# Layer 0's dense stage: the smaller of norm and limit multiplied into the dots in PSUM, not into the cells in SBUF

## What is computed

```python
Wh = h @ W + b
row, col = (edge_index[0], edge_index[1])
sc = jax.nn.softplus(deg_coeff[0] * deg_v + deg_coeff[1])
dot = jnp.sum(Wr * Wc, axis=-1)          # Wr = Wh[row], Wc = Wh[col]
sim = dot / jnp.maximum(nr * nc, EPS)
sim_pos = jax.nn.relu(sim)
sim_neg = -jax.nn.relu(-sim)
base = adj_v * sc * no_diag
prop_pos = jax.ops.segment_sum((base * sim_pos)[:, None] * Wc, row, num_segments=n_nodes)
prop_neg = jax.ops.segment_sum((base * sim_neg)[:, None] * Wc, row, num_segments=n_nodes)
return scale * (coeff[0] * prop_pos + coeff[1] * prop_neg + coeff[2] * Wh)
```

## Time and profile before

| | before |
|---|---|
| median of 3 runs | 5141.49 us (5140.48 to 5144.65) |
| the profiled execution, own time | 5139.28 us |
| its span | 5137.5 us |
| busy PE / DVE / ACT / POOL | 2720.2 / 3940.7 / 789.2 / 3541.7 us |
| chain that ended last, by engine | POOL 39%, issue 19%, PE 17%, DVE 13%, DMA 8% |
| chain, by line, L735 (`add0`) | 16% |

### The profile page before, as it was taken

The page is one execution under the profiler, slowest core; times in us unless marked ns, Lnnn a source line. Parts: engine busy times, 40 slices in busy tenths (PEclk is TensorE's granted clock), DMA queues, the critical chain, the costliest instruction groups (busy, mean ns, idle before and its releaser), DMA issues.

```text
span 5137.5 us, 62046 instructions
## 1 busy us (share of the span) xinstructions
PE 2720.2 (53%) x10695; PEld 1352.5 (26%) x10695; DVE 3940.7 (77%) x10565; ACT 789.2 (15%) x2017; POOL 3541.7 (69%) x3645
## 2 busy tenths in 40 slices
PE   5844266436775000013544444456787777729992
PEld 4532122104665000002211111132333333313331
DVE  8866999646999986646777777755788878789993
ACT  0000022210000025521222222220000000003331
POOL 4777777754777877777777777756777777715562
PEclk9999987668999555557677766678889998869996
DMA  9420167413222146635888888837999999928980
GB/s 350 147 90 9 46 225 256 143 64 118 54 52 54 41 136 203 202 88 197 277 286 290 284 281 287 289 124 252 311 310 305 311 310 311 308 96 311 331 317 21
DMA packets 458298, 1038.77 MB, mean 202 GB/s; under 512 B 129582, under 2 KB 247830, under 8 KB 428141
## 3 DMA queue, kind: packets, MB, share of 16 engines
q1 hardware_dynamic: 167594, 579.38, 31.4%
q0 software_dynamic: 131968, 217.09, 15.0%
q10 hardware_dynamic: 158658, 241.42, 13.5%
HBM read 559.03 MB, written 476.15 MB: 201 GB/s over the span
## 4 chain that ended last, share of the span: by engine, by line
POOL 39%; issue 19%; PE 17%; DVE 13%; DMA 8%; DVEq 1%; ACT 1%; POOLq 0%; SPq 0%; ACTq 0%
POOL arena L696 22%; POOL weights L735 16%; DMA arena<-tab,ring 7%; PE psum L1308 6%; PE psum L1309 5%; PE psum L1389 3%; DVE arena L2242 1%; DVE arena L1698 1%; DVE arena L2069 1%; DVE arena L1963 1%; DVE arena L2073 1%; DVE arena L2055 1%; DVE arena L1848 1%; DMA ring<-meta 1%; DVE arena L2171 1%
## 5 line engine op out<-in xcount | busy, mean ns | idle before, releaser
L696 POOL DMA_INDIRECT arena<-tab,ring x2352 | 2311.3, 983 | 717.3 <-issue 701.5
L1308 PE MATMUL psum<-arena,ident 128*128 128x512 f32 x1176 | 745.2, 721 | 799.6 <-DMA arena<-tab,ring 523.6
L1698 DVE SCALAR_TENSOR_TENSOR arena<-arena,ns 128x64 f32<-128x64 f32 (+2 forms) x2351 | 870.0, 370 | 192.9 <-ACT arena L934 53.0
L735 POOL DMA_INDIRECT weights<-arena x784 | 805.4, 1027 | 291.4 <-issue 238.7
L1309 PE MATMUL psum<-arena,ident 128*128 128x512 f32 x1176 | 687.8, 671 | 0.0
L1308 PEld LDWEIGHTS psum<-arena,ident 128*128 128x128 f32 x1176 | 251.7, 227 | 1184.0 <-issue 993.2
L805 POOL TENSOR_TENSOR arena<-arena,score 128x256 f32<-128x256 f32 x294 | 230.6, 809 | 256.8 <-issue 125.0
L1389 PE MATMUL psum<-arena,ident 128*128 128x512 f32 x784 | 361.4, 607 | 63.9 <-DVE arena L2242 63.5
L2171 DVE SCALAR_TENSOR_TENSOR arena<-psum,rowb 128x1024 f32<-128x1024 f32 x196 | 239.1, 1220 | 200.7 <-PE psum L1309 200.1
L1309 PEld LDWEIGHTS psum<-arena,ident 128*128 128x128 f32 x1176 | 262.7, 223 | 357.4 <-issue 357.4
L1272 PE MATMUL psum<-agg,arena 128*128 128x200 bf16 x2352 | 236.6, 251 | 118.5 <-DVE arena L1821 118.5
(11 more groups left out here) (416 smaller groups left out, 4131.9 us busy)
## 6 DMA issues: line engine op xcount, KB each, us to landing
put<-zero SPq DMA_DIRECT2D x98, 1040.0 KB
arena<-put SPq DMA_DIRECT2D x98, 1040.0 KB
spill<-arena ACTq DMA_DIRECT2D x98, 1024.0 KB, 5.7
arena<-spill SPq DMA_DIRECT2D x98, 1024.0 KB
state<-arena ACTq DMA_DIRECT2D x147, 512.0 KB, 4.7
weights<-zero SPq DMA_DIRECT2D x32, 1600.0 KB, 18.4
arena<-weights SPq DMA_DIRECT2D x32, 1600.0 KB, 7.6
put<-zero SPq DMA_DIRECT2D x14, 3584.0 KB
```

The costliest lines, as they stand in the source:

```text
L696: pool.indirect_dma_start(out=rows[:, h, k, :], out_offset=None, in_=table[:, :], in_offset=bass.IndirectOffsetOnAxis(ap=ring[:, h, word + ...
L735: pool.indirect_dma_start(out=weights0[:, :], out_offset=bass.IndirectOffsetOnAxis(ap=words0[:, g, k:k + 1], axis=0), in_=words0f[:, g, K ...
L1308: pe.matmul(place, lhsT=ident[:, :], rhs=rows_of[0][:, s, columns, 0:width], start=True, stop=False)
L1698: beats.add(dve.scalar_tensor_tensor(out=rows[:, s, k, :], in0=before, scalar=mark(ns, g, k), in1=rows[:, s, k, :], op0=ALU.mult, op1=ALU. ...
```

## The change

The multiplication by the smaller of `per_src` and `limit` is moved from the cells to the dots. The instruction keeps its form and its size; its second tensor and its output are now the PSUM banks with the bent dots. It stands behind `bend0` of the same quarter and waits for it, and `similarity0` waits for it. The wait for the loaded cells moves from the first `weigh0` of a tile to the first `similarity0`.

```diff
-            def weigh0(at, c):
-
-                place, columns = at % 3, slice(c * NP // 4, (c + 1) * NP // 4)
-                if c == 0:
-                    dve.wait_ge(cells_in[place], at // 3 * 16 + 16)
-                dve.scalar_tensor_tensor(out=cells[:, place, columns], in0=per_src[:, columns], scalar=limit[:, ORDER[at]:ORDER[at] + 1],
-                                         in1=cells[:, place, columns], op0=ALU.min, op1=ALU.mult).then_inc(weighted, 1)
-
...
+            def weigh0(at, c):
+
+                dve.wait_ge(bent, at * 4 + c + 1)
+                dve.scalar_tensor_tensor(out=dots_of(c), in0=halves_of(per_src[:, c * NP // 4:(c + 1) * NP // 4]), scalar=limit[:, ORDER[at]:ORDER[at] + 1],
+                                         in1=dots_of(c), op0=ALU.min, op1=ALU.mult).then_inc(weighted, 1)
 
             def similarity0(at, c):
 
-                weights = cells[:, at % 3, c * NP // 4:(c + 1) * NP // 4].rearrange("p (b n) -> p b n", b=2)
+                weights = halves_of(cells[:, at % 3, c * NP // 4:(c + 1) * NP // 4])
+                if c == 0:
+                    dve.wait_ge(cells_in[at % 3], at // 3 * 16 + 16)
                 dve.wait_ge(weighted, at * 4 + c + 1)
-                dve.wait_ge(bent, at * 4 + c + 1)
                 dve.tensor_tensor(weights, weights, dots_of(c), ALU.mult).then_inc(work0, 1)
 
             for at in range(TILES):
-                weigh0(at, 0)
                 for c in range(4):
                     bend0(at, c)
-                    if c < 3:
-                        weigh0(at, c + 1)
+                    weigh0(at, c)
                     similarity0(at, c)
```

More of the change, by code:

```diff
@@ L1738, in _, with halves_of @@
                 tally.done(dve.tensor_copy(weights, bias), wa_set)
-            def weigh0(at, c):
-                place, columns = at % 3, slice(c * NP // 4, (c + 1) * NP // 4)
-                if c == 0:
-                    dve.wait_ge(cells_in[place], at // 3 * 16 + 16)
-                dve.scalar_tensor_tensor(out=cells[:, place, columns], in0=per_src[:, columns], scalar=limit[:, ORDER[at]:ORDER[at] + 1],
-                                         in1=cells[:, place, columns], op0=ALU.min, op1=ALU.mult).then_inc(weighted, 1)
             def dots_of(c):
                 return psum[:, 4 + c % 2 * 2:6 + c % 2 * 2, 0:NP // 8]
+            def halves_of(rows):
+                return rows.rearrange("p (b n) -> p b n", b=2)
             def bend0(at, c):
@@ L1755, in bend0 @@
                 dve.scalar_tensor_tensor(out=dots_of(c), in0=dots_of(c), scalar=sc[:, 11:12],
-                                         in1=signed[:, c % 2, :].rearrange("p (b n) -> p b n", b=2), op0=ALU.mult, op1=ALU.max).then_inc(bent, 1)
+                                         in1=halves_of(signed[:, c % 2, :]), op0=ALU.mult, op1=ALU.max).then_inc(bent, 1)
+            def weigh0(at, c):
+                dve.wait_ge(bent, at * 4 + c + 1)
+                dve.scalar_tensor_tensor(out=dots_of(c), in0=halves_of(per_src[:, c * NP // 4:(c + 1) * NP // 4]), scalar=limit[:, ORDER[at]:ORDER[at] + 1],
+                                         in1=dots_of(c), op0=ALU.min, op1=ALU.mult).then_inc(weighted, 1)
             def similarity0(at, c):
-                weights = cells[:, at % 3, c * NP // 4:(c + 1) * NP // 4].rearrange("p (b n) -> p b n", b=2)
+                weights = halves_of(cells[:, at % 3, c * NP // 4:(c + 1) * NP // 4])
+                if c == 0:
+                    dve.wait_ge(cells_in[at % 3], at // 3 * 16 + 16)
                 dve.wait_ge(weighted, at * 4 + c + 1)
-                dve.wait_ge(bent, at * 4 + c + 1)
                 dve.tensor_tensor(weights, weights, dots_of(c), ALU.mult).then_inc(work0, 1)
             for at in range(TILES):
-                weigh0(at, 0)
                 for c in range(4):
                     bend0(at, c)
-                    if c < 3:
-                        weigh0(at, c + 1)
+                    weigh0(at, c)
                     similarity0(at, c)
```

## The result

The changed kernel takes 5092.62 us (median of 4 runs, 5086.51 to 5097.68), the kernel before beside it 5140.98 us. The ratio is 0.9903, with a 95% interval of 0.989 to 0.9915: faster by 1%. The prediction was 5097.6 us. The profiled execution took 5091.21 us, with a span of 5089.5.

A forecast was written before the change was run, and what follows sets the result against it. POOL's scatter plus three tiles was taken to set the dense stage's end, DVE having much to spare. 5139.28 - 44.9 (hold gone) + 1 (tail) = 5095.4, median 5097.6 us; own range 5092 to 5104, 8 in 10 for 5089 to 5109.

The forecast's parts named there:

- POOL held by `weigh0`: Dense stage: scatters starting inside the old `weigh0`, both tensors in SBUF, wait for its end; all 44.9 us of excess goes.
- The form without a row: The new `weigh0` on DVE, SBUF first, PSUM second and out, not in the trace: taken as 1056 ns.
- The dependent chain: DVE's three operations of a quarter, each waiting for the one ahead: 1.16 + 1.16 + 0.93 = 3.25 us.
- The wait for ACT: DVE waiting in each tile for the dots of quarter 3 through PE and ACT: 0.1 to 0.8 us.
- What hides it: DVE's 26 us more over 29 tiles is covered by one wait for cells, some 40 us; limit 14.9 us a tile.
- After the last scatter: From the cells' landing to the end of the last sums, 40.5 us before: 0 to 4 us lost, 1 taken.
- Sum: Whole kernel: 5139.28 - 44.9 + 1 = 5095.4 us for the profiled execution, median 2.2 above: 5097.6.
- Nothing gained: Rival: the new `weigh0` holds POOL as well, last scatter stays at 1113.2; about 5142 us; 7 in 100.
- Slower: Rival: DVE's chain of three becomes the dense stage's bound, over 16.4 us a tile; 5171 us at 17; 3 in 100.

The follow-up runs named there:

- the forms: One kernel with six forms of `weigh0`, by tile, from before to changed, plus 336 more POOL scatters into an unused tensor; 5449.1 us, read from its trace alone.
- e5_small: The changed kernel with a reduction of 160 columns added behind each `similarity0`; 5096.02 us, 0.9912 of the kernel before.
- e6_large: The changed kernel with a reduction of 600 columns added behind each `similarity0`; 5111.52 us, 0.9943 of the kernel before.
- e12_changed_again: The changed kernel run once more with nothing altered; 5089.13 us, 0.9909 of the kernel before.
- e7_last3: The changed kernel, with the old form and order of `weigh0` again behind the last scatter; 5089.73 us, 0.9903 of the kernel before.

## Why the prediction was right

*POOL held by `weigh0`: 44.9 us.* Right, and shown by the forms: the excess is there with two tensors in SBUF in either order, and gone when one of them is in PSUM, wherever the output goes. The picture behind it was too narrow, since a tensor_scalar with one SBUF tensor holds too; the sum does not use it. The prediction lets L1745 end at 901.53, where the next instruction starts; by its own row it ends at 901.62. Of the 44.9 us, 43.8 to 44.5 show between the first and the last scatter: 1051.9 us before, 1008.1 and 1007.4 in the two profiles of the changed kernel.

*The form without a row: 1056 ns.* Measured 1056.

*The dependent chain: 3.25 us a quarter.* Too dear. `bend0` to `weigh0` is 1.09 us, and so is `weigh0` to `similarity0` in three quarters of four; a quarter without a wait for ACT is mostly 3.09. The 1.16 stands only in quarter 0, in all 30 tiles without a wait for cells: there `similarity0` waits for two semaphores, `weighted` and `cells_in`. So does the `similarity0` of the earlier trace rows that the 1.16 was read from, with `weighted` and `bent`. The wait for ACT was 26.4 us in all, 0.8 for a tile on average, at the upper end of what I gave, and up to 1.19 in a single tile, above it. The two errors nearly cancel, and not by luck: the dots of quarter 3 set the time, and a DVE that comes sooner waits longer, as `e5_small` shows from the other side. With the waits for cells taken out, a tile took (1117.8 - 646.35 - 45.8) / 32 = 13.3 us against my 13.4. The rule of the Trainium skill (VectorE: DVE Perf Modes, "The DRAIN you can't avoid") that a semaphore after each operation costs nothing extra does not hold for this chain, 1.09 against 0.97, but by less than I had it.

*What hides it.* Right, and shown by `e5_small` and `e6_large`: there is cover at 13.6 us for a tile and none at 15.14, so the limit lies between them, where the prediction has 14.9. The waits for cells were two, not one, of 45.8 us together; the other is 1.8 us, and in `e12_changed_again` there is only the long one.

*After the last scatter: 0 to 4 us lost.* 41.6 us against 40.5 in the first profile, so 1.1 lost; 39.1 in the second, so 1.4 won. The 40.5 of before is one profile too. The two profiles of the changed kernel differ in when PE comes back to its full clock, and a loss of 1 was not to be known better than to these few microseconds.

*Sum.* By the profiles the stage gave 42.0 us, by my sum 43.9. The time fell by 48.4 us, by my sum 43.4. The 6 us between lie behind the stage, and the change isn't shown to be their cause. From the start of L1243 to the end of the span the same code takes 3972.9 us in the kernel before, and in the changed one and its variants 3966.8, 3975.2 (`e5_small`), 3972.6 (`e6_large`), 3967.6 (`e7_last3`) and 3966.0 (`e12_changed_again`). They spread over 9 us with the same instructions. Between the profiles of before and of the change, the lead is 41 us up to layer 1's scans (their first starts at 1649.1 and 1607.8), 39 in layer 2 (L2055, later L2056: 2404.8 and 2365.7), 45 where layer 3 begins and 48 at its end (L2171, later L2172: first starts 3536.1 and 3490.9, last ones 4534.0 and 4486.0). So it is won and lost again in stages that the diff does not touch. What makes them vary stays open. With the stage alone the median would have been 5140.98 - 42.0 = 5099.0, above my 5097.6; that it lies 5 us below it, near the lower end of my own range, is luck and not the sum's merit.

*The rivals.* "Nothing gained" is out by the forms and by the scatters of the changed kernel, wherever POOL's scatters run beside the stage. "Slower" did not come true in the runs of the common pace, but its mechanism did at the slower pace, where the order alone cost 0.3 to 0.5% with nothing of POOL to win. The prediction had not asked on what the overlap of POOL and DVE rests.

## What to carry to other kernels

When a chain that ends last runs through GpSimd's indirect DMAs, set their durations beside the Vector instructions in which they start; a mean above the median (here 1091 against 958 ns) can be a hold, and here no list of waits named it. The cure in this case was not fewer Vector instructions but other operands: one tensor in PSUM in the place of a second in SBUF, and no tensor_scalar at double pace beside them. Such a gain is worth what the two engines overlap, and where they do not overlap, the longer chain of dependent instructions is all that is left of the change.

## What the hardware showed that I had not expected

- A tensor_scalar with one SBUF tensor holds GpSimd's DMA too: 42 ns for each scatter with four of 628 ns in a tile, somewhat below the 50 to 80 of the rival set down ahead of that run.
- The same program took 5141 us beside some runs and 7670 to 7718 us beside others, half as long again, and with that another engine bounds the stage.
- PE's clock at short idle times: in the first profile of the changed kernel dots that came after 1.83 us of idle time ran in 0.94 us, the next ones, after another 2.21 us, in 1.71, which is the lower of the two clocks, 1.2 GHz; the last sums of all, after 2.67 us, again at full speed. The length of the idle time alone does not tell the clock. Before the 2.21 us PE had run 0.94 us since its last pause, before the 2.67 us it had run from 1107.42 to 1115.19 without one; that this made the difference was not tested. Timeline and granted clock (the column before the last two) in the changed kernel:

```profile
1104.27 0.94 PE L1226 MATMUL psum<-arena 64*128 64x400 f32 x4 [1.83 <-DVE arena L1766]
...
1107.42 1.71 PE L1226 MATMUL psum<-arena 64*128 64x400 f32 x4 [2.21 <-DVE arena L1766]
```

```profile
1107.40:1109.00 1.60, 1.57 (x4) 0.50 (x4) 1.56 (x2) 0.00 (x0) 0.00 (x0) 0.50 0.00 0
1117.80:1120.70 2.90, 2.84 (x16) 1.06 (x16) 0.01 (x1) 0.00 (x0) 0.00 (x0) 1.00 0.00 0
```
